# Attention over the edges of a graph network: 392 edges in a row per partition in place of 128 edges across partitions

## The reference

```python
q, k, v = (einsum('ni,hid->nhd', x, W) + b)      # 128 features each, 8 heads
e = edge_attr[:, None, None] * We                # one weight per edge
alpha = einsum('ehd,ehd->eh', q[dst], k[src] + e) / sqrt(d)
m = segment_max(alpha, dst)
ex = exp(alpha - m[dst])
denom = segment_sum(ex, dst)
agg = segment_sum(ex / denom[dst] * (v[src] + e), dst)
out = layernorm((agg + x @ Wskip) @ Wo + bo + x)
```

## Time and profile before

| | us |
|---|---|
| median of 3 timed executions | 1717.68 |
| lowest and highest | 1715.59, 1720.96 |
| span of the profiled execution, first to last instruction | 2214.6 |
| of it: `front`, the table of the first layer (no edges yet) | 19 to 67 |
| of it: `front`, counts of edges by TensorE | 67 to 490 |
| of it: `front`, edges | 490 to 942 |
| of it: `layers` and `middle` | 942 to 1414 |
| of it: `edges_attention` | 1414 to 2121 |
| of it: `tail_nodes` | 2121 to 2215 |

### The profile page before, as it was taken

One profiled execution on the slowest core, in us unless ns is written; L12 is line 12 of the kernel. 1 busy time (PEld: TensorE's weight loads), 2 busy tenths in 40 slices (PEclk: granted clock), 3 DMA queues, 4 the chain that ended last, 5 costly groups with the idle time before them and its releaser, 6 DMA issues. The chain is left out here.

```text
span 2214.6 us, 31367 instructions
## 1 busy us (share of the span) xinstructions
PE 1322.1 (60%) x7890; PEld 1079.8 (49%) x7890; DVE 1066.3 (48%) x2950; ACT 944.2 (43%) x2004; POOL 1037.5 (47%) x1171
## 2 busy tenths in 40 slices
PE   3222146666676689799989997314444454434666
PEld 2100013444554578688989895214433453424555
DVE  4411149873443467554964315314444454433666
ACT  0100137774454468275536645413333343333424
POOL 5677710005566640024458441665565666556234
PEclk9555569988888789999989998657676777667787
DMA  5221212224565563074545451546667666666521
GB/s 147 70 66 53 68 55 104 90 99 152 166 197 162 169 211 101 11 252 164 194 136 208 147 209 49 162 135 172 172 184 197 199 187 197 177 169 176 157 67 43
DMA packets 214072, 314.19 MB, mean 142 GB/s; under 512 B 31232, under 2 KB 159743, under 8 KB 213818
## 3 DMA queue, kind: packets, MB, share of 16 engines
q1 hardware_dynamic: 110724, 153.96, 21.9%
q0 software_dynamic: 33488, 81.02, 13.0%
q10 hardware_dynamic: 69734, 77.65, 10.9%
HBM read 223.87 MB, written 88.67 MB: 141 GB/s over the span
## 5 line engine op out<-in xcount | busy, mean ns | idle before, releaser
L374 POOL DMA_INDIRECT fr_ring<-table,src_i x392 | 376.2, 960 | 405.5 <-SPq L655 277.7
L1765 POOL DMA_INDIRECT e_kv<-kv_table,e_idx x392 | 387.1, 987 | 269.0 <-DVE e_msg L1848 153.7
L685 PE MATMUL fe_ps<-fe_space 128*128 128x400 bf16 x591 | 176.0, 422 | 244.5 <-issue 151.9
L685 PEld LDWEIGHTS fe_ps<-fe_space 128*128 128x128 bf16 x591 | 86.0, 145 | 334.3 <-issue 309.2
L776 DVE TENSOR_SCALAR fe_space<-fe_space,fr_key 128x400 bf16<-128x400 f16 x591 | 157.5, 323 | 176.1 <-remote 77.7
L1004 POOL CAST ly_af<-ly_au 128x640 fp32r<-128x640 uint16 x240 | 163.4, 729 | 126.4 <-DVE ly_part L1409 61.0
L1779 PE MATMUL e_q<-e_qs,e_mask 128*128 128x136 f32 x784 | 148.1, 360 | 80.9 <-issue 48.2
L1831 ACT ACTIVATE e_row<-e_p 128x864 f32<-128x864 f32 x56 | 49.6, 885 | 336.4 <-remote 292.5
L731 ACT ACTIVATE fe_space<-fe_ps 128x800 uint16<-128x800 f32 x100 | 83.6, 836 | 255.8 <-PE fe_ps L685 140.0
L707 PE MATMUL fe_ps<-fr_ring,fe_space 128*128 x976 | 147.9, 294 | 61.7 <-issue 32.3
L1779 PEld LDWEIGHTS e_q<-e_qs,e_mask 128*128 128x128 f32 x784 | 135.6, 258 | 87.9 <-issue 81.2
(11 more groups left out here) (397 smaller groups left out, 3177.2 us busy)
## 6 DMA issues: line engine op xcount, KB each, us to landing
ly_au<-edge_counts SPq DMA_DIRECT2D x88, 800.0 KB, 4.5
sums_att<-e_row ACTq DMA_DIRECT2D x56, 532.0 KB
q_starts<-fe_space SPq DMA_DIRECT2D x56, 476.0 KB
e_qs<-q_starts SPq DMA_DIRECT2D x56, 476.0 KB
fe_edge<-in_edgesT ACTq DMA_DIRECT2D x98, 256.0 KB
edge_counts<-fe_space ACTq DMA_DIRECT2D x25, 800.0 KB
e_drow<-dst_short SPq DMA_DIRECT2D x56, 224.0 KB
fr_ring<-table,src_i POOLq DMA_INDIRECT x392
```

Of the source, the lines that this page charges most:

```text
L374: pool.indirect_dma_start(f.ring[:, n % RB, t, 0:D], None, tab[0][:, :], bass.IndirectOffsetOnAxis(ap=src_i[:, at:at + 1].bitcast(U32), ax ...
L685: nc.tensor.matmul(ps[:, bass.ds(at, NW)], left(n), right(n % IS), start=False, stop=True, skip_group_check=True).then_inc(c["item"], 1)
L1765: pool.indirect_dma_start(kv[s][:, t, :], None, kv_table[:, :], bass.IndirectOffsetOnAxis(ap=idx[s][:, t:t + 1].bitcast(U32), axis=0)).the ...
```

## The change

The edges are laid out the other way. Partition p holds the 392 edges p*392 to p*392+391 in a row, and a block is seven edges of each partition. The edges of a node then stand along the free axis of one partition, but for those that cross from a partition to the next (127 borders in place of 391).

- The masks, `dh`, `drow`, the index loads, all of TensorE's work and the copies from PSUM are gone from `edges_attention`. `middle` loads `src_i`, `w_col` and `dst_i` in the new layout; `front` therefore stores `src_flat` in place of `dst_short`, later in its chain, and `w_flat`, which TensorE turns first.
- VectorE spreads q by seven `fill` instructions per block, each q row plus `follows` (1 where an edge has the destination of the one before) times the row before it; it sums the messages by seven `add` instructions of the same kind on `row`, which carries on from the block before. Both are scalar_tensor_tensor, over 136 and 144 numbers.
- The running maximum is two scans over 8 heads x 8 columns (the seven edges and the carried one); ScalarE's `carried` copies the last maximum over. A second exponential, `dec`, rescales the carried sum.
- VectorE's order in a step is written out by `block_step`; no part of the stage is a loop any more.
- `qfirst` is one indirect DMA in place of four and is issued behind the gathers of block 0.
- `tail_nodes` works on 128 borders in place of 392: `z` is 128 x 128, one pass of TensorE each, the scans run over 128 columns, and `head` comes by an indirect DMA ahead of the row gathers.

```diff
 in front:
-                        dve.tensor_copy(dst_16[:, :].bitcast(U16), dst_t[:, :, :].rearrange("n t e -> n (t e)")).then_inc(cut, 1)
...
                         after(dve.tensor_copy(src_t[:, :, :], ps_t[0:NF, 0:TF * P].rearrange("n (t e) -> n t e", e=P)))
+                        dve.sem_inc(cut, 1)
...
+                        for k in range(TF):
+                            turned_w = nc.tensor.transpose(ps_b[0:NF, k * P:(k + 1) * P], w_col[:, k::TF], ident[:, :])
+                        turned_w.then_inc(w_turned, 1)
...
 in middle:
+                        sp.dma_start(src_i[:, :], chunks(src_flat)).then_inc(edges_in, 16)
+                        sp.dma_start(w_col[:, :], chunks(w_flat)).then_inc(edges_in, 16)
+                        sp.dma_start(dst_i[:, :], chunks(dstflat[1:EP + 1])).then_inc(edges_in, 16)
...
 in edges_attention, GpSimd:
+                        for n in range(NB):
+                            c.free(pool, "exv", n, KS)
                             for t in range(TB):
...
+                                pool.indirect_dma_start(kv[n % KS][:, t, :], None, kv_table[:, :],
+                                                        bass.IndirectOffsetOnAxis(ap=src_i[:, at:at + 1].bitcast(U32), axis=0)).then_inc(gathered[n % KS], 16)
+                            if n == 0:
+                                pool.wait_ge(first_known, 1)
+                                pool.indirect_dma_start(qfirst[:, :], None, q_table[:, :],
...
 in edges_attention, VectorE:
+                        def fill(n, t):
...
+                            dve.wait_ge(c["fill"], at)
+                            before = qs[(at - 1) // TB % QS][:, (t - 1) % TB, :]
+                            dve.scalar_tensor_tensor(here, before, follows[:, at:at + 1], here, ALU.mult, ALU.add).then_inc(c["fill"], 1)
+                        def add(n, t):
...
+                            here, above = row[n % RR][:, t + 1, 0:MW], row[n % RR][:, t, 0:MW]
+                            dve.scalar_tensor_tensor(here, above, follows[:, at:at + 1], here, ALU.mult, ALU.add).then_inc(c["sum"], 1)
+                        def block_step(n):
+                            s, k4 = n % KS, n % 4
+                            dve.wait_ge(gathered[s], (n // KS + 1) * TB * 16)
+                            dve.wait_ge(c["fill"], (n + 1) * TB)
+                            dve.tensor_tensor(prod[:, :, :], qs[n % QS][:, :, 0:D], kv[s][:, :, 0:D], ALU.mult).then_inc(c["prod"], 1)
+                            dve.tensor_tensor(wq[:, :, :], qs[n % QS][:, :, D:QW], weights(n), ALU.mult).then_inc(c["wq"], 1)
+                            fill(n + 1, 0)
+                            dve.tensor_reduce(red[:, :, :]...)
+                            add(n - 1, 0)
+                            dve.tensor_tensor(by_head(al[k4][:, :])[:, :, 1:CB], red..., wq..., ALU.add)
+                            fill(n + 1, 1)
...
+                            dve.tensor_tensor_scan(fs[k4][:, :], brk[:, n, 0:H * CB], al[k4][:, :], -BIG, ALU.add, ALU.max).then_inc(c["fs"], 1)
+                            add(n - 1, 1)
...
+                            dve.tensor_tensor_scan(bs[k4][:, ::-1], brk[:, n, H * CB:0:-1], fs[k4][:, ::-1], -BIG, ALU.add, ALU.max).then_inc(c["bs"], 1)
+                            fill(n + 1, 2)
+                            dve.tensor_tensor(dif[k4][:, :], al[k4][:, :], bs[k4][:, :], ALU.subtract).then_inc(c["dif"], 1)
+                            add(n - 1, 2)
+                            for t in range(3, TB):
+                                fill(n + 1, t)
+                                add(n - 1, t)
+                            c.ready(dve, "ex", n)
+                            dve.tensor_tensor(row[n % RR][:, 1:CB, D + H:MW], row[n % RR][:, 1:CB, D:D + H], weights(n), ALU.mult)
+                            dve.tensor_tensor(wide(row[n % RR][:, 1:CB, 0:D]), wide(kv[s][:, :, D:2 * D]), ...).then_inc(c["exv"], 1)
...
+                            (two multiplies by dec into row[n % RR][:, 0, :], then_inc(c["carry"], 1))
...
 in tail_nodes:
-                                dve.tensor_tensor(z[:, n, :, :], iota[0:TP, :].unsqueeze(1).broadcast_to([TP, TK, P]),
-                                                  key_rel[:, n, :].unsqueeze(2).broadcast_to([TP, TK, P]), ALU.is_equal).then_inc(c["z"], 1)
+                                dve.tensor_scalar(z[:, n, :], iota[:, :], key_rel[:, n:n + 1], None, ALU.is_equal).then_inc(c["z"], 1)
...
-                                for k in range(TK):
-                                    last = nc.tensor.matmul(ps_n[g % 3][:, i * RW:(i + 1) * RW], z[:, n, k, :], scaled[:, k, :], start=(k == 0), stop=(k == TK - 1))
+                                last = nc.tensor.matmul(ps_n[g % 3][:, i * RW:(i + 1) * RW], z[:, n, :], scaled[:, :], start=True, stop=True)
```

More of the change, by code:

```diff
@@ L74 @@
 NC = -(-E // HEAVY)
[L75 to L123, removed]
+assert NB % KS == 0 and KS % QS == 0 and KS % RR == 0 and NT % NS == 0 and EP >= E and ET == TK * TP
 class Front:
@@ L206, in gnn_kernel @@
         q_starts = dram("q_starts", [EP + NP, QW])
-        dst_short = dram("dst_short", [EP], U16)
+        src_flat = dram("src_flat", [EP], I32)
+        w_flat = dram("w_flat", [EP])
         sums_att = dram("sums_att", [EP + P, RW])
@@ new lines, in ring @@
+                def ring(name, shape, slots):
+                    return [tensor(f"{name}{s}", shape) for s in range(slots)]
+                c = Counts(sem, "e4", "fill prod wq red al col fs bs dif ex m exw exv carry sum")
+                gathered = [sem(f"e4_gathered{s}") for s in range(KS)]
+                landed = [sem(f"e4_landed{s}") for s in range(QS)]
+                stored = [sem(f"e4_stored{s}") for s in range(RR)]
+                bounded, numbered, first_known, picked, next_in = (sem(f"e4_{k}") for k in "bounded numbered first_known picked next_in".split())
@@ L1728, in _ @@
                     def _(sp):
-                        c.credit(sp)
-                        def index(n, s, r):
-                            if not (isinstance(r, int) and r == 0):
-                                wait_rows(sp, s, r - 1, TB)
-                            c.hold(sp)
-                            with nc.allow_non_contiguous_dma(reason="seven sources per partition"):
-                                sp.dma_start(idx[s][:, :], srccol[:, bass.ds(n * TB, TB)]).then_inc(indexed[s], 16)
@@ L1750, in _ @@
-                        pipelined(sp, NB, KS, [(0, index), (4, load)])
-                        for s in range(KS):
-                            sp.wait_ge(stored[s], NB // KS * 16)
+                        dst_at = chunks(dstflat[1:EP + 1])
+                        with nc.allow_non_contiguous_dma(reason="one number per partition"):
+                            sp.dma_start(bounds[:, 4:5], dst_at[:, 0:1]).then_inc(bounded, 16)
+                            sp.dma_start(bounds[:, 0:1], dst_at[:, ET - 1:ET]).then_inc(bounded, 16)
+                            sp.dma_start(bounds[0:P - 1, 1:2], dst_at[1:P, 0:1]).then_inc(bounded, 16)
+                            sp.dma_start(bounds[0:P - 1, 2:3], dst_at[1:P, ET - 1:ET]).then_inc(bounded, 16)
+                            sp.dma_start(bounds[0:P - 2, 3:4], dst_at[2:P, 0:1]).then_inc(bounded, 16)
```

441 lines of the change are left out of this document (191 added, 250 removed).

## The result

| | before | after |
|---|---|---|
| median of the timed executions, us | 1719.32 | 1841.24 |
| lowest and highest | 1715.59, 1721.74 | 1839.37, 1842.85 |
| ratio | | 1.072 (95% interval 1.0698 to 1.0742) |
| span of the profiled execution | 2214.6 | 1840.1 |

A forecast was written before the change was run, and what follows sets the result against it. Timed attention was taken as paced by POOL's issue of 392 gathers at 1.29 us. Attention +26, tail -10, front and middle +1 make +17: 1735 us, range 1688 to 1785.

The forecast's parts named there:

- In the profile TensorE's results are announced late while gathers are issued: Front and attention: late TensorE results explain the profiled span of 2214.6 us against the timed 1717.7.
- Rival 2: Attention: TensorE's lateness is in timed runs too; 1685 us if 50 us of it are, 1559 in full; chance 0.07.
- Timed attention is paced by POOL's issue of 392 gathers: Attention before the change: gathers at 1.29 us each, 9.0 us a block, 531 us together with start and drain.
- What VectorE gets: Attention: VectorE's work per block after the change, 7.2 us, fitting beside 9.0 us of gathers; bounds 9.1 and 10.0.
- rival 3: Attention: VectorE becomes the bound at 10.0 us a block, 1758 us, or 1806 with long POOL delay (chance 0.16).
- What it does to POOL: Attention: VectorE's two-input instructions delay each gather by 0.12 us; 557 us against 531, +26.
- The upper bound of 0.3: Attention: largest delay allowed per gather, 0.3 us, if POOL settles into step with VectorE's long multiplies.
- half the formula: Attention before: measured gather delay 0.03 us where the random-fall formula gives 0.06; that ratio gives 0.07 to 0.085 after.
- Rival 1: Attention: POOL hardly waits for VectorE; at zero delay attention takes 510 us, the kernel 1688; chance 0.24.
- Rival 4: Attention: VectorE and POOL block each other, 7 gathers x 0.96 added to VectorE, 13.9 us a block, 1976 us; chance 0.02.
- Rival 5: Attention: instruction fetch lags as the loop is written out in full, 1 us a block, 1790 us; chance 0.03.
- Tail, -10: Tail: smaller one-hots, fewer TensorE passes and shorter scans save 10 us, bounds -3 and -14; tail at 80 to 87 us.

The follow-up runs named there:

- b2: The kernel before, unchanged, profiled a second time: 1714.2 us, profiled span 1712.4 us.
- b1: The kernel before with an eighth indirect DMA (gather) in each block of attention, into a spare tile: 1782.4 us, ratio 1.038 to the kernel before.
- x7: The changed kernel with the block's messages and the spread q in PSUM in place of SBUF: 1681.1 us, ratio 0.981 to the kernel before.
- x2: The changed kernel with one copy of one number per partition on VectorE ahead of the score product: 1842.5 us.
- x3: The changed kernel with four more scalar_tensor_tensor with two SBUF inputs put behind each block's last add: 1903.2 us.
- x5: The changed kernel in which, from a block's fourth fill on, each fill and add waits for the one ahead, inputs left in SBUF: 1711.6 us.
- x1: The changed kernel with five small one-input copies put into VectorE's dense run of fills and adds in each block: 1739.9 us.
- x4: The changed kernel with the block's messages in PSUM, so adds read one input there: 1695.0 us, ratio 0.988 to the kernel before.
- x8: The changed kernel with spare TensorE matmuls behind each block from the 45th on, ending within some 6 us of the tail: 1843.5 us.

## Why the prediction was wrong, by its own steps

- **"In the profile TensorE's results are announced late while gathers are issued", and not in timed runs: right.** b2 has the same kernel at a span of 1712.4. Of the 502 us that the first profile was longer, 335 lie ahead of attention (1414 against 1079) and 167 in it. The extra time was in that one execution. That late announcements made it up is read from that profile's rows alone, and what caused them was not tried. Rival 2, which had it in the timed runs, falls.
- **"Timed attention is paced by POOL's issue of 392 gathers", 531 us: right, 9 us low.** Its budget had a slip: 413 less 222 is 191 and not 185, so it reads 501 to 541 us. Measured it is 540: a gather takes 1000 ns there, not 987, and 1.20 us per added gather (b1) bears the pacing out.
- **"What VectorE gets", 7.2 us a block: low by 1.0.** From L1748 at 1301.43 to the end of L1786 at 1309.59 it is 8.16 us. Fills and adds follow each other at 0.275 us, not at the 0.21 of the tail's neighbours, and 14 x 0.065 = 0.9. It was no bound all the same: rival 3 (VectorE the bound at 10 us) falls with the 187 us that VectorE waits.
- **"What it does to POOL", 0.12 us a gather: the step that failed.** It was named as the term that decides, and its direction and cause were right; its size is 0.41 (1365 ns less the 954 of an undisturbed gather, x7). Two parts of the argument were wrong. First the unit: "a gather that falls at random into an instruction of length L waits L/2". It waits to the end of the chain. From the fifth fill to the end of L1776 the chain is 2.86 us; taken as one L over the 9.7 us of the forecast, the prediction's own formula would have given 2.86 x 2.86 / (2 x 9.7) = 0.42 for this term alone. That this is so near the measured 0.41 is chance: the formula takes random places, and with the block's real 11.75 us it gives 0.35. The overlap of neighbours had been read in the rows and used, but only to make VectorE cheap. Second, "at random": the gathers don't fall at random, the wait at the second scan brings them to the same place in 53 of 56 blocks (x2). With 0.41 in place of 0.12 the step's own sum is 393 x (0.957 + 0.30 + 0.41) + 16 = 671 us; the profile shows 671 (1079.5 to 1750.7).
- **The upper bound of 0.3 was no bound.** It came from single long multiplies. x3 has 0.56 (1517 - 954), with a chain that is four instructions longer. With the bound of 0.3, 1806 us stood in the text under rival 3 and was left out of the range at 1785.
- **Calibration by the kernel before, "half the formula".** 0.03 to 0.05 was measured there, in a kernel where L1848 has only one short instruction with two SBUF inputs ahead of it (L1846), and L1855 behind it reads PSUM. A ratio from single instructions says nothing about a chain.
- **Rival 1, no delay, "510 us" of attention: the place where x7 stands.** From 1078.8 to 1588.8 it is 510.0. So with its inputs placed so that nothing waits, the layout is worth 30 us of attention against the kernel before; the delay cost 161.
- **Rival 4, the two block each other, 0.96 us of VectorE for each gather: false at that size.** L1748 and L1776 take 1093 and 1081 ns beside a POOL that is 80% busy. A hold on VectorE is there, but it is some 0.06 us (x5: a fill takes 0.41 us in place of 0.36 and an add 0.43 in place of 0.37 where a gather starts 0.06 to 0.12 us into it). The Trainium skill (SBUF — State Buffer, Who interferes with whom) says that a VectorE instruction with two SBUF inputs contends with a GpSimd instruction that reads SBUF: x1, x4 and x7 agree, 1365 ns against 954. It says that the pair is held for the whole instruction: where VectorE comes first, the runs show POOL kept out for more than that, a chain of instructions; where POOL comes first, they show VectorE held for some 0.06 us of a gather's 0.95. Rival 5 (code fetch) falls too: 0.30 us of issue per gather, as before.
- **Tail, -10: it is -4, inside the bounds of -3 to -14, though at 89.1 us outside the 80 to 87 named as its sign.** VectorE lost 10 us of busy time (70.5 to 60.1), with the one-hots at 315 ns (L1955) where 200 were forecast. TensorE's busy time hardly fell, 64.7 to 63.3, with a quarter of the passes in L1890: the granted clock is 0.50 in place of 0.76, and a matmul of L1907 takes 502 ns, where its like in the second profile of the kernel before (L2007) takes 361. So slower matmuls ate what the fewer passes saved in TensorE's busy time; that this cost the tail its missing 6 us is argued, not shown.
- **Front and middle, +1: it is 0** within a microsecond (1078.8 against 1079.5 for POOL's first DMA of attention).
- **"The span falls to about 2055":** it fell to 1840, since the extra time of the first profile was gone from the front as well.

The sum with the measured terms: +132 - 4 + 0 = +128 by the spans (1712.4 and 1840.1), +122 by the medians.

## What to carry to other kernels

Where GpSimd issues indirect DMAs on the critical path, look along VectorE's order for chains of instructions with two SBUF inputs that start before the one ahead has ended: a gather that meets one can be kept out to the chain's end, and a block whose steps are locked to the gathers meets it nearly every time. Not every such border keeps a gather out, so read the long gathers and what ends with them from the timeline. Break the chain (an instruction with an input in PSUM, or a wait for the one ahead), or better, put one input of each in PSUM when TensorE leaves it free. And before an estimate is summed against a profile, ask whether its span agrees with the timed median; where it doesn't, a second profile is worth more than an argument.

## What the runs showed that was not expected

- VectorE keeps POOL out over instruction borders: 3.78 us over eight instructions (the changed kernel), 4.90 over twelve (x3), and a break of some 0.04 us between them ends it (x5: at most 1.69). At borders earlier in the block a gather gets in within 0.2 us (1.01 to 1.15 beside the second scan), though the instructions there overlap and have two SBUF inputs too. Why those borders let it in and those in the chain do not was not settled: in the one block of the changed kernel in which the gather started 0.08 us into the fourth add instead of 0.20 to 0.22, it got in and took 1.11 us, and the next one, 0.11 us into the seventh fill, took 2.49.
- A gather holds VectorE too, for some 0.06 us (x5), so the exclusion works both ways, but very unequally.
- TensorE's granted clock was 1.00 in the 10 us up to the end of its work in attention and 0.50 from the tail's first matmuls to the end (x8): the two levels, 2.4 and 1.2 GHz, with a pause of 6 us in TensorE's work between.
- One and the same kernel gave profiled spans of 2214.6 and 1712.4 us, at a timed 1717.
